# Second stage of a two-part kernel: gelu kept in PSUM, turned by DMA, part of the centring moved off VectorE

## The reference

```python
def act_quant_fake(x):
    scale = 127.0 / jnp.clip(jnp.max(jnp.abs(x), axis=-1, keepdims=True), 1e-05)
    return jnp.clip(jnp.round(x * scale), -128.0, 127.0) / scale
def weight_quant_fake(w):
    scale = 1.0 / jnp.clip(jnp.mean(jnp.abs(w)), 1e-05)
    return jnp.clip(jnp.round(w * scale), -1.0, 1.0) / scale
def bitlinear(x, w, b):
    return jnp.einsum('btd,hd->bth', act_quant_fake(x), weight_quant_fake(w)) + b
h = layernorm(x, ln1_g, ln1_b)            # 256 columns
h = bitlinear(h, w1, b1)                  # 256 -> 1024
h = jax.nn.gelu(h, approximate=False)
h = layernorm(h, ln2_g, ln2_b)            # 1024 columns
h = bitlinear(h, w2, b2)                  # 1024 -> 256
x = x + _L0_xattn_ref(_layernorm(x), ctx, ...)
x = x + _L0_ffn_ref(_layernorm(x), ...)
```

## Time and profile before

| | |
|---|---|
| median of 3 runs | 1086.9 us (1085.64 to 1095.88) |
| the profiled execution's own time | 1081.3 us |
| its span, first to last instruction | 1079.8 us |
| mean granted TensorE clock | 0.985 of full |
| busy: PE, DVE, ACT, POOL | 939.9, 958.6, 949.8, 720.1 us |
| first part, second part | gelus begin at 585.4 us |

### The profile page before, as it was taken

How to read it: one execution, slowest core, us unless ns; L and a number is a source line. 1 busy time by engine, 2 the same in 40 slices (tenths; PEclk the granted TensorE clock), 3 DMA queues, 4 the chain that set the end, 5 groups by cost and what they waited for, 6 DMA issues and landing times. The chain is left out here.

```text
span 1079.8 us, 27074 instructions
## 1 busy us (share of the span) xinstructions
PE 939.9 (87%) x8371; PEld 606.0 (56%) x8371; DVE 958.6 (89%) x1265; ACT 949.8 (88%) x2590; POOL 720.1 (67%) x1051
## 2 busy tenths in 40 slices
PE   6999999999999999999998478777777877787775
PEld 4666666666666666666664244444444444444444
DVE  2688888888888888888888899999999999999996
ACT  5788999999899999999978679999999999999993
POOL 3366666777666666666675667777777777777775
PEclk9999999999999999999999789999999999999998
DMA  6599977678856666666653112233223323332334
GB/s 171 138 177 192 185 167 165 164 163 167 165 160 170 164 164 176 163 162 164 162 128 89 44 26 35 35 39 39 31 37 39 39 30 38 39 36 32 39 40 69
DMA packets 145136, 114.48 MB, mean 106 GB/s; under 512 B 52376, under 2 KB 135576, under 8 KB 145072
## 3 DMA queue, kind: packets, MB, share of 16 engines
q1 hardware_dynamic: 127488, 96.77, 38.1%
q0 software_dynamic: 16864, 16.26, 12.5%
q10 hardware_dynamic: 720, 0.66, 0.2%
HBM read 71.62 MB, written 33.63 MB: 97 GB/s over the span
## 5 line engine op out<-in xcount | busy, mean ns | idle before, releaser
L721 DVE TRANSPOSE_TENSOR_REDUCE nm_part<-banks 128x64 f16<-128x2048 f32 x64 | 147.6, 2306 | 2.6 <-PE banks L1281 2.2
L1053 ACT ACTIVATE g_dev<-g,g_sum 128x1024 bf16<-128x1024 f32 x128 | 149.2, 1166 | 0.0
L1058 ACT ACTIVATE g<-banks,h_dq 128x1024 f32<-128x1024 f32 x128 | 142.4, 1130 | 4.5 <-PE banks L1214 2.5
L1006 ACT ACTIVATE probs<-banks 120x512 f32<-120x512 f32 x256 | 132.2, 604 | 14.7 <-PE banks L1311 11.3
L1369 PE MATMUL banks<-wo_sb,o_t 128*128 128x256 f32 x512 | 135.3, 399 | 1.7 <-DVE o_t L741 1.3
L1244 PE MATMUL banks<-w_t,g_t 128*128 128x256 bf16 x1008 | 122.4, 275 | 11.8 <-ACT g_t L1091 9.1
L1208 PE MATMUL banks<-w_t,h_t 128*128 128x512 bf16 x504 | 123.7, 390 | 1.9 <-ACT g L1058 1.9
L1244 PEld LDWEIGHTS banks<-w_t,g_t 128*128 128x128 f16 x1008 | 94.4, 98 | 50.1 <-issue 27.3
L1360 PE MATMUL banks<-xt,wq_c 128*128 128x256 f32 x512 | 121.3, 380 | 0.0
L523 POOL COPY h_dq<-h_cl 128x2 f32<-128x2 f32 (+1 forms) x64 | 14.3, 223 | 140.9 <-DVE h_qs L784 139.8
L1369 PEld LDWEIGHTS banks<-wo_sb,o_t 128*128 128x128 f32 x512 | 87.1, 190 | 36.8 <-ACT log_sum L995 26.0
(11 more groups left out here) (170 smaller groups left out, 2584.7 us busy)
## 6 DMA issues: line engine op xcount, KB each, us to landing
x_in<-in_x SPq DMA_DIRECT2D x64, 256.0 KB, 4.7
xt<-in_x_t SPq DMA_DIRECT2D x64, 256.0 KB, 4.1
xr<-in_x SPq DMA_DIRECT2D x64, 256.0 KB, 4.3
out<-xr SPq DMA_DIRECT2D x64, 256.0 KB, 6.2
out<-res POOLq DMA_DIRECT2D x62, 256.0 KB, 4.4
ctx_t<-in_ctx_t SPq DMA_DIRECT2D x64, 128.0 KB, 3.7
r_bc<-r_rows SPq DMA_DIRECT2D x63, 128.0 KB, 4.1
w_raw<-in_w_t SPq DMA_DIRECT2D x8, 256.0 KB
```

The lines of the kernel that those rows point to most:

```text
L721: dve.tensor_reduce(nm_part[:, :, 0:C * RB], blocks_p, AX.X, ALU.max, negate=True, apply_transpose=True).then_inc(max_done, 1)
L1006: act.activation(probs[:, p, j, :, :], sc_p[0:KV, j, :, :], ACT.Exp, scale=SCALE).then_inc(probs_done, 1)
L1053: act.activation(g_dev[:, t, :], g[:, p, t, :], ACT.Square, scale=-float(F), bias=g_sum[:, p, t:t + 1], accum_out=g_ssq[:, p, t:t + 1]).th ...
L1058: act.activation(g[:, p, t, :], u_p[t], ACT.Gelu, scale=h_dq[:, b, t:t + 1], accum_out=g_sum[:, p, t:t + 1]).then_inc(gelu_done, 1)
```

## The change

- **Gelu in place.** `gelu` writes back to `u_p[t]` in PSUM; the SBUF tile `g` goes. The square and the centring read PSUM. `rows_up` may overwrite a tile only when VectorE has centred it and ScalarE has squared it, and is now issued one batch ahead, tile by tile.
- **Last 256 columns.** ScalarE writes g + mean of columns 768 to 1023 to `part` (an Identity with a bias), GpSimd multiplies by the gain (`gain_part`). VectorE centres the first 768. ScalarE's order per tile becomes gelu, mean, identity, square.
- **Offset from PSUM.** A copy of the offset row is put into banks 0 and 1 once, and from batch 4 on the affine reads it there.
- **Scales.** No reciprocal on VectorE: GpSimd raises four columns to powers -0.5 and -1 in one instruction; ScalarE divides the maximum by 127 (`step_size`).
- **Quantising and turning.** GpSimd writes integers plus 1536 as f16 to `nq`; it works on batch j-2 and doesn't wait for VectorE's affine of the same turn. SP issues two transposing DMAs of 128x1024 per batch into `g_t` (four buffers). TensorE's transposes and ScalarE's copies stay for the last four batches alone. The down product comes four batches behind, the residual five, the store six.
- **Seam and end.** The hand-written orders at the seam and behind the loop are rewritten to fit.

The core of the diff:

```diff
@@ sync
+                def ffn(j, n):
+                    b, p = j - 2, n % 2
+                    after(sp, y2_ps, b - 3)
+                    for t in range(T):
+                        sp.wait_ge(gq_done, b * T + t + 1)
+                        sp.dma_start(g_t[:, b % 4, t, :, :], nq[:, p, t, :], transpose=True).then_inc(g_turned[p], 16)
+                steps(sp, 2, NB - 2, FFN_L0, NB - 6, ffn, 4)
@@ gpsimd
+                    pool.tensor_scalar(nq[:, p, t, :], gn[r][:, t, :], scale, HALF_ONE, ALU.mult, ALU.add).then_inc(gq_done, 1)
+                def gain_part(b, t, n):
+                    pool.wait_ge(part_centred, b * T + t + 1)
+                    pool.tensor_tensor(gn[n][:, t, F - PART:F], part[:, n % 2, t, :],
+                                       g2_bc[:, F - PART:F], ALU.mult).then_inc(part_done, 1)
+                def scales(b, p):
+                    pool.wait_ge(g_affine, (b - 1) * T)
+                    pool.wait_ge(gve_done, b + 1)
+                    pool.wait_ge(gmx_done, b - 1)
+                    pool.tensor_tensor(g_rq[:, p, :], g_vm[:, p, :], powers[:, :], ALU.pow).then_inc(gr_done, 1)
                 def ffn(j, n):
+                    gain_part(j, 0, n)
+                    b = j - 6
                     if live(b, NB):
+                        store(b, (n + 2) % 4)
+                    gain_part(j, 1, n)
+                    scales(j, n % 2)
+                    quantise_batch(j - 2, (n + 2) % 4)
@@ vector
+                def centre(j, t, n):
+                    dve.wait_ge(ssq_done, j * T + t + 1)
+                    dve.scalar_tensor_tensor(out=gn[n][:, t, 0:F - PART], in0=u_p[t][:, 0:F - PART], scalar=g_nm[:, n % 2, t:t + 1],
+                                             in1=g2_bc[:, 0:F - PART], op0=ALU.add, op1=ALU.mult).then_inc(g_centred, 1)
+                def affine(j, n):
+                    offset = b2n_bc[:, :] if isinstance(j, int) and j < 4 else b2n_p
...
+                def ffn(j, n):
+                    centre(j, 0, n)
+                    largest_rows(j - 1, (n + 3) % 4)
+                    centre(j, 1, n)
+                    affine(j, n)
@@ scalar
                 def deviation(b, t, p):
                     act.wait_ge(gelu_done, b * T + t + 1)
+                    act.activation(g_nm[:, p, t:t + 1], g_sum[:, p, t:t + 1], ACT.Copy, scale=-1.0 / F).then_inc(gnm_done, 1)
+                    act.wait_ge(gnm_done, b * T + t + 1)
+                    act.activation(part[:, p, t, :], u_p[t][:, F - PART:F], ACT.Identity,
+                                   bias=g_nm[:, p, t:t + 1]).then_inc(part_centred, 1)
+                    act.activation(g_dev[:, t, :], u_p[t], ACT.Square, scale=-float(F),
                                    bias=g_sum[:, p, t:t + 1], accum_out=g_ssq[:, p, t:t + 1]).then_inc(ssq_done, 1)
+                def step_size(b, r):
+                    after(act, gr_done, b + 1)
+                    act.wait_ge(g_maxed, b + 1)
+                    act.activation(g_vm[:, r % 2, T:2 * T], g_max[:, r, :], ACT.Copy, scale=1.0 / QMAX).then_inc(gmx_done, 1)
                 def ffn(j, n):
+                    for t in range(T):
+                        gelu(j, t, p)
+                        deviation(j, t, p)
+                    variance(j, p)
+                    b = j - 2
                     if live(b, NB):
+                        step_size(b, (n + 2) % 4)
                     b = j + 3
                     if n % 2 == 1 and live(b, NB):
                         bias_turned(b, n // 2)
+                    b = j - 5
                     if live(b, NB):
+                        for t in range(T):
+                            residual(b, t, (n + 3) % 4)
@@ tensor
                 def rows_up(b, n):
                     for t in range(T):
-                        after(pe, gelu_done, (b - 1) * T + t + 1)
+                        pe.wait_ge(g_centred, (b - 1) * T + t + 1)
+                        pe.wait_ge(ssq_done, (b - 1) * T + t + 1)
                 def ffn(j, n):
+                    b = j + 1
                     if live(b, NB):
+                        rows_up(b, (n + 1) % 4)
+                    b = j - 4
                     if live(b, NB):
+                        batch_down(b, n)
@@ tensor, behind the loop
+                for t in range(T):
+                    turn_late(NB - 4, t)
+                turn_late(NB - 3, 0)
+                for t in range(T):
+                    late_down(NB - 4, t, y2_other, t == 0)
...
```

More of the change, by code:

```diff
@@ L258, in xattn_ffn @@
         floor_set = sem("floor_set")
-        g_inverted = sem("g_inverted")
-        gqs_done = sem("gqs_done")
+        gmx_done = sem("gmx_done")
+        powers_set = sem("powers_set")
+        part_centred = sem("part_centred")
+        part_done = sem("part_done")
+        b_placed = sem("b_placed")
+        g_turned = [sem(f"g_turned{p}") for p in range(2)]
         gdq_done = sem("gdq_done")
@@ L577, in out_scale, with quantise_rows, quantise_batch @@
                                        ALU.mult).then_inc(gdq_done, 1)
-                def quantise_rows(t, r):
+                def quantise_rows(t, r, scale):
                     p = r % 2
-                    pool.tensor_scalar(gn[r][:, t, :], gn[r][:, t, :], g_qs[:, p, t:t + 1], MAGIC_H,
+                    pool.tensor_scalar(nq[:, p, t, :], gn[r][:, t, :], scale, HALF_ONE,
                                        ALU.mult, ALU.add).then_inc(gq_done, 1)
+                def quantise_batch(b, r):
+                    pool.wait_ge(gr_done, b + 3)
+                    if isinstance(b, int) and b == 0:
+                        pool.wait_ge(w_out_done, 1)
+                    if isinstance(b, int) and b == NB - 2:
+                        pool.wait_ge(gt_ps, T)
+                    else:
+                        after(pool, g_turned[r % 2], 16 * (b - r % 2))
+                    out_scale(b, r)
+                    for t in range(T):
+                        quantise_rows(t, r, g_rq[:, r % 2, T + t:T + t + 1])
@@ L1452, in _, with turn_late @@
[L1452 to L1455 removed]
+                def turn_late(b, t):
+                    pe.wait_ge(gq_done, b * T + t + 1)
+                    turn_gelus(b, t)
@@ new lines, in late_down @@
+                def late_down(b, t, y, first):
+                    pe.wait_ge(gt_done, (b - NB + 4) * T + t + 1)
+                    rows_down(b, t, y, b % 4, first)
+                pe.wait_ge(g_centred, NB * T)
+                pe.wait_ge(ssq_done, NB * T)
+                for t in range(T):
+                    turn_late(NB - 4, t)
+                turn_late(NB - 3, 0)
+                for t in range(T):
+                    late_down(NB - 4, t, y2_other, t == 0)
+                correct(bank[3].rearrange("p (t n) -> p t n", t=T))
@@ new lines, in _ @@
+                turn_late(NB - 3, 1)
+                pe.wait_ge(out_done, (NB - 4) * T)
+                for t in range(T):
+                    late_down(NB - 3, t, y2_tiles, t == 0)
+                correct(y2_p)
+                pe.wait_ge(g_affine, NB * T)
+                for t in range(T):
+                    turn_late(NB - 2, t)
+                pe.wait_ge(out_done, (NB - 3) * T)
+                late_down(NB - 2, 0, y2_other, True)
+                turn_late(NB - 1, 0)
+                late_down(NB - 2, 1, y2_other, False)
```

318 lines of the change are left out of this document (123 added, 195 removed).

## The result

Before 1089.02 us, after 1108.36 us (medians of four runs each): ratio **1.0187, 95% interval 1.0142 to 1.0233**. The profiled execution of the changed kernel has a span of 1106.2 us, against 1079.8; its mean granted clock is 0.919, against 0.985. The spans lie 26.4 us apart and the medians 19.3, so some 7 us between the two profiles are scatter between executions.

What follows compares the result with a forecast made beforehand. VectorE bounds the kernel at 7.23 us a batch; after the change ScalarE would, at 7.35, +7 us over 59 periods, offset by the head. With +3 us of tail on 1081.3 and 5.6 to the median: 1090 us, range 1071 to 1116.

Steps and rivals of the forecast that it cites:

- rival B: TensorE's clock falls because of a pause between the two tiles' products in every batch; +29 us, 1119 us; chance 0.13.
- TensorE loses its transposes: TensorE in each batch: its transposes go, 0.62 us a tile.
- The pause that I worked out: TensorE between the two tiles' products: 3.13 us apart, 1.4 of it work, so a pause of 1.7 in every batch.
- the excess: TensorE's work at the low clock, 8.8 us a batch, over 7.35; a third of it priced, +0.5 x 59 = +29.
- the middle part at no change and the tail at +3: Last affine ends at 1065.3 against 1065.55 us; down products behind the loop make the tail 13 to 15 against 10.4.
- rival E: VectorE's PSUM operands cost what fewer columns save: 7.2 us a batch, still 1090; chance 0.56 together with the forecast.
- ScalarE as the bound at 7.35: ScalarE's queue in the steady part takes 7.35 us a batch, against 7.23 before; over 59 periods +7 us.
- The wait of the mean for the gelu's own sum: ScalarE per tile: gelu until its sum has landed 1.24 us, plus 0.09 before the mean starts.
- Rival A: ScalarE is cheaper and the head stays warm: 7.10 us a batch, 1072 us; chance 0.24.
- Rival C: GpSimd still blocked by an affine with its offset in PSUM: 8.4 us a batch, +62, 1152 us; chance 0.02.
- Rival D: Transposing transfers one by one, +121 us, 1211, or gelu at half pace in one bank, +118, 1208; chance 0.05.
- The comparison with 639: Head: the fifth batch's gelu was to start near 619 to 623 us instead of 639.

Runs made afterwards that it cites:

- warm_b: Changed kernel plus six idle matmuls between the two tiles' up products per batch, and ScalarE's copy of the turned bias moved behind its residuals; 1.0101 to the kernel before.
- part128: Changed kernel with 128 instead of 256 columns for ScalarE and GpSimd; ratio 1.0257 to the kernel before, 1108.6 us.
- offset_sbuf: Changed kernel with the affine's offset read from SBUF in all batches; ratio 1.0571 to the kernel before, 1143.6 us.
- warm6: Changed kernel plus six idle matmuls between the two tiles' up products in batches 4 to 59, bias turned later; ratio 1.0262 to the kernel before.
- warm_mix: Changed kernel plus four idle matmuls before each batch's first up product and six between the two in every second batch; ratio 1.0077 to the kernel before.
- fill_short: Changed kernel plus four idle matmuls ahead of the first tile's up product only, the 1.53 us pause staying; ratio 1.0421 to the kernel before.

## Why the prediction was right in its parts and wrong in its likeliest case

The time lies within the range, but for the reason of rival B, which had 0.13, and not for the forecast's 1090. The range held it because it took in the nearer part of B. That B was priced at 1119 and came out nearer is in part luck, as its price was a guess at a third of an excess.

**What failed**: "TensorE loses its transposes" was costed at nothing, and the argument against rival B, that at 78% busy the clock never fell, took a share where the order of work mattered: the clock fell with TensorE busy 83% and held at 78%. Before, TensorE's pauses were 1.1 and 0.5 us, each followed by transposes; after, 0.86 and 1.53. The pause that I worked out, 1.7, was measured at 1.53, but in about every second batch, not in each, since at the low level it closes. Nor does TensorE decide for most of the time, as B has it: it makes ScalarE wait in one batch of four. I priced the excess at 0.5 a batch; measured: the four undisturbed periods, 7.10, 7.38, 7.24 and 7.45 (the last where the clock held), average 7.29, and the mean was 7.61, so 0.32 a batch, over 58 periods **19 us of the 26 us** between the profiled spans. warm_b shows that this is the clock's doing: the same batches take 7.1 to 7.7 us when it is held.

**The whole account** of those 26.4 us: first gelu 4.6 later (scatter, see above); from there to the end of the last affine 498.9 (1088.86 - 589.97) against 480.2 us, 18.7; from there to the end of the last residual 12.9 against 10.4, 2.5; the rest 0.6. I had put the middle part at no change and the tail at +3. The middle part hides a gain: first to sixth gelu is 3.5 longer and the 58 periods from there 20.8, but from the last gelu to the end of the last affine it is 10.2 us instead of 15.9.

**VectorE**: 0.94 a centring (0.93), maximum 2.20, affine pair 2.40 to 2.5. PSUM operands cost nothing visible (rival E fell). It was relieved as reckoned, and hides its gain behind ScalarE.

**ScalarE as the bound at 7.35**: 7.29. From one gelu to the next of a pair it takes 3.00 without a wait. The wait of the mean for the gelu's own sum was over-charged (the mean starts 1.23 after the gelu, not 1.33), the identity 0.37 for 0.36, the squares 1.09 and 1.29 for 1.09 and 1.32; I had left out that batches with a bias copy (7.38 and 7.45) are 0.2 to 0.3 longer than those without (7.10 and 7.24), not 0.16. part128 shows that this queue decides: 0.2 less in it is 0.2 less in the undisturbed period. Rival A's 7.10 is the shortest batch, not the mean. In-place gelu runs at full pace, with its sum started after 0.99 as before (1.00). By an estimate from the Trainium skill ("Perfetto Trace Analysis", section "Optimizing Scalar/DVE Operations") writing PSUM takes 0.04 off. The instruction's length has it (1.09 instead of 1.13 us in the mean), the spacing, which sets the period, hasn't.

**GpSimd**: power 1.03 (1.0 taken), gain multiplications 0.76 (0.7), 6.1 busy a batch (6.0). Rival C fell, and offset_sbuf shows what it would have been (1143.6 us on its chip, priced at 1152).

**DMAs**: the issue doesn't scale with columns: 1.24 us for 1024 of them against 1.20 for 512. They landed in 3.3 us in the median, and TensorE waited for the result 1.0 us in all. Rival D fell.

**Head**: behind the first gelu, shifted by its 4.6, the fifth came at 622.1, between the 619 to 623 expected. The comparison with 639 was a slip: since gelus run ahead of the affine, the gelu at 639.4 in the kernel before is the seventh's, and the fifth's started at 618.6. Reckoned over the last affine, as the sum was, the slip had no weight.

**What stays open**: why long and short falls take turns; why pauses of 1.6 us did no harm in warm6, and why pauses of 1.1 us did none before the change, while warm_mix lost the clock behind some of 0.89; and how much of the head's 3.5 us (first to sixth gelu 47.3 against 43.8) is the clock, which stood at 0.50 from 607 to 643 us. In that stretch TensorE had pauses of 1.7 to 4.8 us. No run was made for any of these.

## What to carry to other kernels

When work is taken off TensorE, list the pauses that this leaves in its queue before counting the saving, and give the chance of a fallen clock a fair price: here neither the busy share nor the longest pause told beforehand whether the clock would hold. Runs with idle matmuls in one pause and then in the other show where they help. Here they helped between the two up products, if they displaced nothing, a small copy of a bias included; ahead of the first product alone they did harm. And while one batch in four was held by such a stall, a cut in the bounding engine's queue (part128) didn't show.

## What was not expected of the hardware

- The granted clock fell to 0.50 and came back twice in four batches (30.6 us), one short fall and one long one, over most of the steady part, with TensorE over 80% busy and no pause above 1.55 us. With less idle time but the same longest pause (fill_short) it fell as often, and long falls were more frequent. With pauses as long in another place (warm6) it fell twice in 390 us.
- One PSUM operand in place of the SBUF one on VectorE makes GpSimd's quantising 1.12 instead of 1.78 us, its tiny scale 0.20 instead of 0.71 and VectorE's own operation 1.28 instead of 1.50 us.
- A transposing DMA took nearly the same time to issue for 512 and for 1024 columns (1.20 and 1.24 us).
